# Both halves of a chunk's diagonal products in a row, cumulative sums in column halves, and a new order of steps

## The chip, the cores and the metric

The kernel runs on one core of one Trainium2 chip. The metric is the device time of one execution, in microseconds (us). The program is one launch; the weights are laid out beforehand with their contracted dimension first.

## What is computed

One block of a network on an input of 2 batches x 2048 tokens x 512 features, all in float32. A small product of a condition with `wmod` gives shifts, scales and gates for each batch. Then come a mixer and a feed-forward, each on a normalized and modulated input and added back through a gate:

```python
h = layernorm(x) * (1 + ca) + sa
x = x + ga * mixer(h)
h = layernorm(x) * (1 + cb) + sb
x = x + gb * (silu(h @ Wg) * (h @ Wu)) @ Wd     # integer weights, widened and scaled

# mixer: zxbcdt = h @ W_in.T; x, B, C through a causal convolution of 4 taps and silu
Y_diag = einsum('bcln,bcsn,bhcls,bcshp->bclhp', C, B, L, X)    # L = exp of differences of cumsum(dt*A)
Y_off  = einsum('bcln,bchpn,bhcl->bclhp', C, states, exp(A_cumsum))
y = (Y_diag + Y_off + Dp * X) * silu(z);  y = rmsnorm(y) * norm_w;  out = y @ W_out.T
```

The mixer has 16 heads of 64 features, a state of 128 per head, and an inner width of 1024. The kernel works in chunks of 128 tokens.

## The kernel before

**Stages.** `mixer_stage` handles 4096 tokens in 16 tiles of 256 tokens (two chunks of 128), the two batches taking turns. The first step (`first`) runs the setup and the projections of tile 0. Then come 15 turns, `turn(n, b)` for n = 1 to 15; each projects tile n (calls guarded by `own`), finishes tile u = n - 1 (guarded by `bef`) and prepares the input of tile n + 1 (guarded by `nxt`). The last tile is finished in `drain`, mixed with the first products of the feed-forward, and the feed-forward follows (`FeedForward`).

**Order.** Each engine has its own list of steps, written out by hand in `first`, `turn` and `drain` of its block, and runs it strictly in that order. Between engines there are semaphores; each step waits for counts (`wait(eng, sem, n, per, c)` waits for n * per + c).

**TensorE's list in a turn.** `scores_G` (the B, C products of both chunks, one bank `small`), `project_zdt` (2), `project_tile` (10; 12 float32r products of 256 columns each), `project_z` (4), and for the chunks c = 0, 1 of tile u: `transpose_x`, `transpose_B`, two `y_off` (a half f of 8 heads each, bank `yoff`), two `y_diag` (bank `ydiag`), two `states` (bank `state`), `transpose_g`, `project_out`. `cumulate` multiplies dt*A with a triangle and with ones for the cumulative sums. A full-precision float32 product is issued as two MATMUL instructions.

**y_diag** already works in column halves: each head's 128 output rows are computed as two products of 64 rows, at the tile positions (0, 0) and (0, 64), 32 instructions for a half of 8 heads. Both halves go to the bank `ydiag`, so the second half waits until VectorE has read the first (`read_ydiag`, L1124 to L1128). In the old list `project_tile` 0 and 1 stand between the halves of chunk 0; `cumulate`, `project_tile` 8, `project_out`, `project_tile` 9 and `y_off(1, 1)` between those of chunk 1. `y_diag(0, 0)` and both last `y_diag` of the chunks stand behind or before steps of full width.

**VectorE's list in a turn.** `mask_G`, four `scores` (decay times masked B, C products, 128x1024), four `read_yoff`, `decay_S`, `read_ydiag` and `read_state`, two `decay_X`, two `gate`, 30 `conv` (three taps of ten tiles), 17 small steps of `softplus` that end in `dtA`, `sums` (reads `cumulate`'s result), `stats`, `norm`, `split_h`, `low_g`, and four `diff` (8 operations each on the broadcast sums). `states(c, 1)` on TensorE waits for `read_state(c, 0)`; `cumulate` waits for `dtA`; `project_zdt(n + 1, c)` waits for `split_h`.

**ScalarE** evacuates banks (`evac_tile`, `evac_x`, `evac_g`, `silu_z`, `scale_out`) and computes silu and exp. **GpSimd** multiplies X with D and adds the residual. **SyncE's queue** stores the sums to memory and broadcasts them back over the partitions, 1 MB for each chunk (L548); the broadcast of chunk 1 stands behind the store of x1 of chunk 0 and the load of the next residual rows, which follows `project_out(0)`.

## Time and profile before

| | |
|---|---|
| median of 3 runs | 1459.25 us (1459.07 to 1463.02) |
| the profiled execution | 1463.41 us, of which the span is 1461.7 us |
| TensorE busy | 1430.2 us |
| VectorE busy | 1116.2 us |
| ScalarE busy | 637.5 us |
| mean granted TensorE clock | 0.996 |
| first step and setup | 0 to 74.54 us of the span |
| the 15 turns | 74.54 to 927.21 us |
| drain and feed-forward | 927.21 to 1461.7 us |

Busy time is the union of an engine's instructions. Matmul ends are modelled, and matmuls overlap, so the time of a block of them is best read from the start of its first to the start of the next block's first. In lines of the timeline, equal neighbours are merged (x12), and a bracket gives the engine's idle time before them and who ended it. A turn here goes from one `scores_G` (L1481) to the next.

### The profile page before, as it was taken

To read this page: it belongs to the slowest core of one execution; us is meant where nothing else is said; L and a number is where in the kernel's file an instruction comes from. 1 tells how busy PE (TensorE), PEld (TensorE's weight loads), DVE (VectorE), ACT (ScalarE), POOL (GpSimd) and SP (SyncE) were. 2 spreads that over 40 slices of the span, in tenths; PEclk is the share of its full clock that TensorE was granted. 3 is DMA by queue.
4 is the path that set the end of the run, shared out by engine and by line. 5 is a ranking of instruction groups with operands and counts; after the bars stand their busy time and mean duration, and the time that the engine had idled before them with its cause. 6 is when DMAs were issued, how large, how long until landed. Compare 5 with 4: busy or idle time off the path is not lost.

```text
span 1461.7 us, 25392 instructions
## 1 busy us (share of the span) xinstructions
PE 1430.2 (98%) x9369; PEld 1146.0 (78%) x9369; DVE 1116.2 (76%) x2521; ACT 637.5 (44%) x1300; POOL 298.7 (20%) x335
## 2 busy tenths in 40 slices
PE   7999999999999999999999999999999999999998
PEld 3677787787887887877777778779888888888887
DVE  4799998998998999999998999857536455364632
ACT  4565565575575565564655654422212011120210
POOL 1012223213212312322322132121110211101101
PEclk9999999999999999999999999999999999999999
DMA  9413213212222222132132132702210202112010
GB/s 320 151 37 131 88 45 123 87 52 96 94 88 95 68 100 95 41 135 100 39 131 81 51 116 70 292 15 80 73 59 28 87 14 73 39 49 87 8 51 30
DMA packets 56409, 124.99 MB, mean 86 GB/s; under 512 B 6438, under 2 KB 10066, under 8 KB 52188
## 3 DMA queue, kind: packets, MB, share of 16 engines
q1 hardware_dynamic: 55744, 123.27, 24.1%
q8 instruction: 77, 1.26, 0.4%
q14 instruction: 48, 0.39, 0.1%
q10 hardware_dynamic: 540, 0.07, 0.0%
HBM read 97.62 MB, written 25.69 MB: 84 GB/s over the span
## 4 chain that ended last, share of the span: by engine, by line
PE 70%; DVE 19%; issue 7%; POOL 1%; DMA 1%; ACT 1%; DVEq 0%; POOLq 0%; SPq 0%
PE bank L2032 18%; PE bank L1443 17%; PE bank L2062 9%; PE bank L1594 7%; PE bank L1592 6%; DVE xBC L987 5%; PE bank L1532 3%; DVE decay L1079 2%; PE bank L1557 2%; DVE state L1121 2%; PE bank L325 2%; DVE y L1134 1%; DVE X_D L1127 1%; PE bank L1544 1%; DVE X L1097 1%
## 5 line engine op out<-in xcount | busy, mean ns | idle before, releaser
L1867 ACT ACTIVATE silu_gate<-bank,params 128x512 f32<-128x512 f32 (+1 forms) x99 | 63.5, 642 | 366.0 <-PE bank L2032 343.8
L987 DVE SCALAR_TENSOR_TENSOR xBC<-conv_in,wconv,xBC 128x256 f32<-128x256 f32 x480 | 211.9, 474 | 3.3 <-ACT xBC L697 0.4
L1939 DVE SCALAR_TENSOR_TENSOR hidden<-bank,params,silu_gate 128x512 f32<-128x512 f32 (+1 forms) x99 | 68.3, 690 | 125.6 <-PE bank L2032 124.4
L2062 PE MATMUL bank<-W_down,hidden_high 128*128 128x512 f32 x374 | 139.1, 390 | 0.0
L606 POOL TENSOR_TENSOR X_D<-X,Drow 128x1024 f32<-128x1024 f32 x32 | 62.7, 1961 | 352.9 <-ACT X_D L781 315.5
L2032 PE MATMUL bank<-ff_h_high,W_gate 128*128 128x512 f32 (+1 forms) x352 | 132.3, 380 | 0.0
L2032 PE MATMUL bank<-ff_h_high,W_up 128*128 128x512 f32 (+1 forms) x352 | 131.1, 376 | 0.3 <-DVE hidden L1939 0.3
L2032 PE MATMUL bank<-ff_h_low,W_gate 128*128 128x512 f32 (+1 forms) x352 | 131.0, 376 | 0.0
L2032 PE MATMUL bank<-ff_h_low,W_up 128*128 128x512 f32 (+1 forms) x352 | 131.0, 376 | 0.0
L2062 PE MATMUL bank<-W_down,hidden_low 128*128 128x512 f32 x330 | 128.5, 389 | 0.0
L1443 PE MATMUL bank<-h_high,W_in_high 128*128 128x256 f32 x640 | 124.7, 317 | 0.1
L1594 PE MATMUL bank<-W_out,gT 128*128 128x512 f32 x256 | 115.0, 592 | 0.0
L1062 DVE TENSOR_SCALAR decay<-decay,sums 128x128 f32<-128x128 f32 x512 | 106.5, 283 | 0.0
L1443 PEld LDWEIGHTS bank<-h_high,W_in_high 128*128 128x128 f32 x640 | 89.0, 190 | 21.5 <-issue 18.5
L1859 POOL TENSOR_TENSOR ff_x_resid<-ff_branch,ff_x_resid 128x512 f32<-128x512 f32 x32 | 41.3, 1291 | 298.2 <-DVE ff_branch L1970 292.8
L1443 PE MATMUL bank<-h_high,W_in_low 128*128 128x256 f32 x640 | 101.5, 280 | 0.0
L1443 PE MATMUL bank<-h_low,W_in_high 128*128 128x256 f32 x640 | 101.4, 280 | 0.0
L696 ACT ACTIVATE conv_in<-bank 128x256 f32<-128x256 f32 x160 | 61.0, 381 | 88.2 <-PE bank L1443 88.2
L1970 DVE TENSOR_TENSOR ff_branch<-bank,gate_row 128x512 f32<-128x512 f32 x32 | 22.1, 690 | 100.7 <-PE bank L2062 100.7
L1544 PEld LDWEIGHTS bank<-X,decay 128*64 128x64 f32 x2048 | 65.0, 138 | 38.2 <-issue 27.7
L1079 DVE TENSOR_TENSOR decay<-decay,G_masked 128x1024 f32<-128x1024 f32 x64 | 91.9, 1436 | 0.9 <-ACT decay L770 0.4
L697 ACT ACTIVATE xBC<-bank,params,wconv 128x256 f32<-128x256 f32 x160 | 90.2, 564 | 0.0
(196 smaller groups left out, 3276.0 us busy)
## 6 DMA issues: line engine op xcount, KB each, us to landing
decay<-sums_scratch SPq DMA_DIRECT2D x32, 1024.0 KB, 5.2
wq_rows<-wqT SPq DMA_DIRECT2D x33, 256.0 KB, 4.8
widened_scratch<-wq_rows SPq DMA_DIRECT2D x33, 256.0 KB, 3.4
x_tile<-x SPq DMA_DIRECT2D x32, 256.0 KB, 3.1
x_resid<-x SPq DMA_DIRECT2D x32, 256.0 KB, 2.9
x_scratch<-x_resid SPq DMA_DIRECT2D x32, 256.0 KB, 3.0
ff_x_resid<-x_scratch SPq DMA_DIRECT2D x32, 256.0 KB, 4.5
out<-ff_x_resid SPq DMA_DIRECT2D x32, 256.0 KB, 2.0
```

Of the source, the lines that this page charges most:

```text
L697: nc.scalar.activation(A.xc[b][:, m, :], ps[:, 0:SC], ACT.Identity, bias=A.bconv[:, m:m + 1], scale=A.wconv[:, m, 3:4]).then_inc(a_emptied, 1)
L987: nc.vector.scalar_tensor_tensor(A.xc[b][:, m, :], A.raw[:, m, j:j + SC], A.wconv[:, m, j:j + 1], A.xc[b][:, m, :], ALU.mult, ALU.add).the ...
L1062: last = nc.vector.tensor_scalar(A.L[c][:, h, :], A.L[c][:, h, :], A.s3[:, c * H + h:c * H + h + 1], 0.0, ALU.subtract, ALU.min)
L1079: nc.vector.tensor_tensor(x, x, A.Gm[:, c, :].unsqueeze(1).broadcast_to([P, HH, P]), ALU.mult) \
L1443: mm = nc.tensor.matmul(out, lhs(wp, ap), rhs(wp, ap), start=(i == 0), stop=(i == last))
L1544: mm = nc.tensor.matmul(ydiag[s, h * HD:(h + 1) * HD], A.L[c][:, g, s], A.X[:, g * HD:(g + 1) * HD], start=True, stop=True, tile_position= ...
L1592: nc.tensor.matmul(ps[:], gT[gp][:, k, :], Wo[wp][:, k, :], start=(k == 0 and i == 0), stop=False)
L1594: mm = nc.tensor.matmul(ps[:], A.gT[:, k, :], A.Wo[:, k, :], start=False, stop=(k == KI - KH - 1))
L1867: self.nc.scalar.activation(B.sg[m % 2][:, 0:size], self.gates[m % 2][:, 0:size], ACT.Silu, scale=self.T.sgate[:, m:m + 1]).then_inc(self. ...
L1939: nc.vector.scalar_tensor_tensor(hid, self.ups[m % 2][:, 0:size], self.T.sup[:, m:m + 1], B.sg[m % 2][:, 0:size], ALU.mult, ALU.mult).then ...
L2032: mm = nc.tensor.matmul(ps[:, 0:self.TURNS[t][2]], W[:, k, m * P:(m + 1) * P].bitcast(dt), self.h(t, a, k).bitcast(dt), start=(k == 0 and ...
L2062: mm = nc.tensor.matmul(self.downs[c % 2][:], self.hidden_tile(t, a, m)[:, s].bitcast(dt), B.Wd[:, m, :].bitcast(dt), start=(m == 0 and a ...
```

## The change

Three things are done at once.

1. `column_halves` is a helper that issues a product as two of 64 output rows. `y_diag` uses it as before; `cumulate` now uses it for its first two products too, so these have 8 MATMUL instructions of 64 rows in place of 4 of 128 rows. The third product of `cumulate` stays as it was.
2. The second half of `y_diag` writes to the bank `state` instead of `ydiag`, except in `drain`. It waits for the state's reads instead of for `read_ydiag` of the first half, and `states(c, 0)` waits until that bank has been read. Both halves of a chunk now follow each other directly; behind those of chunk 0 stands `transpose_B`, behind those of chunk 1 stands `cumulate`.
3. The lists of steps of TensorE, VectorE and ScalarE have a new order, in `first` and in `turn`. In the turn, `states(1, 1)` on TensorE moves behind `project_out(1)`. On VectorE, `scores(0, 1)` and `scores(1, 0)` move forward, `read_yoff(0, 1)` moves behind `read_ydiag(0, 0)`, `decay_S(0, 1)` behind `gate(0)`, most of the softplus steps stand without other work between them, `sums` moves forward, `norm(0)` and `norm(1)` stand together behind `gate(1)`, `conv` 9's first two taps move among the `diff`, `decay_S(1, 1)` moves just before `read_state(1, 0)`, and `read_state(1, 1)` to the end. On ScalarE, `evac_zdt(0)` comes before `evac_x(0)`, `exp_dt` behind `evac_tile` 2, `evac_x(1)` behind `evac_tile` 5, `measure(0)` behind `silu_z(1)`, and `exp_sums` just before the last `exp_decay`. In `first`, ScalarE scales the rest of W_out (`wout_scale`) before `silu_z(0)` instead of behind `silu_z(1)`, `silu_q` comes earlier and `widen_second` behind the last silu; TensorE's `gate_rows` come before `project_z(0)`, and its second `section` directly behind the first. The queues of SyncE and GpSimd keep their lists.

```diff
+
+
+def column_halves(nc, out, lhsT, rhs):
+
+    for i in (0, P // 2):
+        s = slice(i, i + P // 2)
+        mm = nc.tensor.matmul(out[s, :], lhsT[:, s], rhs, start=True, stop=True, tile_position=(0, i))
+    return mm
...
+        self.section(pe, 1)
         pe.wait_ge(self.const_step, 6)
         self.turn_cols(pe, 0)
-        self.section(pe, 1)
         transpose_ln()
         self.turn_cols(pe, 1)
         pe.wait_ge(self.win_low, 1)
...
+    def ydiag_bank(n, f):
+
+        return state if f and n != N else ydiag
+
...
                 wait(dve, yoff_done, u, 2 * NC, 2 * c + f + 1)
+                wait(dve, e3_done, u, 1, 1)
                 nc.vector.tensor_tensor(heads(A.S[1 - b], f), heads(A.S[1 - b], f), e3(1, c, f),
...
-        def read_ydiag(u, c, f):
+        def read_ydiag(n, u, c, f):
             wait(dve, ydiag_done, u, 2 * NC, 2 * c + f + 1)
             wait(dve, XD_done, u, NC, c + 1)
-            nc.vector.tensor_tensor(A.XD[:, f * W:(f + 1) * W], ydiag[:, 0:W], A.XD[:, f * W:(f + 1) * W],
+            nc.vector.tensor_tensor(A.XD[:, f * W:(f + 1) * W], ydiag_bank(n, f)[:, 0:W], A.XD[:, f * W:(f + 1) * W],
                                     ALU.add).then_inc(ydiag_read, 1)
 
...
@@ -1252,123 +1260,133 @@
             if bef:
                 mask_G(u)
                 scores(u, 0, 0)
+                scores(u, 0, 1)
                 read_yoff(n, u, b, 0, 0)
-                scores(u, 0, 1)
+                decay_S(u, b, 0, 0)
+                scores(u, 1, 0)
+            if own:
+                conv(n, b, 0, 0)
+            if bef:
+                read_ydiag(n, u, 0, 0)
                 read_yoff(n, u, b, 0, 1)
-                decay_S(u, b, 0, 0)
+                decay_X(n, u, 0)
+            if own:
+                dt_first(n, b)
+            if bef:
+                read_ydiag(n, u, 0, 1)
+            if own:
+                conv(n, b, 1, 0)
+            if bef:
+                gate(n, u, b, 0)
+            if own:
+                conv(n, b, 0, 1)
+                conv(n, b, 1, 1)
+            if bef:
                 decay_S(u, b, 0, 1)
-                read_ydiag(u, 0, 0)
...
-            nc.tensor.matmul(small[:, 0:NC * H], A.triu[:], a, start=True, stop=True)
-            nc.tensor.matmul(small[:, NC * H:2 * NC * H], A.ones[:], a, start=True, stop=True)
+            column_halves(nc, small[:, 0:NC * H], A.triu[:], a)
+            column_halves(nc, small[:, NC * H:2 * NC * H], A.ones[:], a)
             mm = nc.tensor.matmul(small[0:NC * H, 2 * P:3 * P], a, A.triu[:], start=True, stop=True)
             mm.then_inc(cs_done, 1)
...
@@ -1536,14 +1554,16 @@
             wait(pe, M_done, u, 2 * NC, 2 * c + f + 1)
             t_wait(pe, t_emptied, n, ("x", c, f), 1)
 
-            wait(pe, ydiag_read, u, 2 * NC, 2 * c + f)
+            ps = ydiag_bank(n, f)
+            if ps is state:
+
+                wait(pe, S_step, u, 4 * NC, 4 * c)
+            else:
+                wait(pe, ydiag_read, u, 2 * NC, 2 * c + f)
             for h in range(HH):
                 g = f * HH + h
-                for i in (0, P // 2):
-                    s = slice(i, i + P // 2)
-                    mm = nc.tensor.matmul(ydiag[s, h * HD:(h + 1) * HD], A.L[c][:, g, s],
-                                          A.X[:, g * HD:(g + 1) * HD], start=True, stop=True,
-                                          tile_position=(0, i))
+                mm = column_halves(nc, ps[:, h * HD:(h + 1) * HD], A.L[c][:, g, :],
+                                   A.X[:, g * HD:(g + 1) * HD])
             mm.then_inc(ydiag_done, 1)
 
         def states(n, u, c, f):
@@ -1553,6 +1573,7 @@
             if f:
                 wait(pe, S_step, u, 4 * NC, 4 * c + 3)
             else:
+                wait(pe, ydiag_read, u, 2 * NC, 2 * c + 2)
                 wait(pe, S_step, u, 4 * NC, 4 * c)
             nc.tensor.matmul(state[:, 0:W], A.Btok[:], A.X[:, f * W:(f + 1) * W],
                              start=True, stop=True).then_inc(state_done, 1)
...
             u = before(n)
@@ -1636,56 +1657,52 @@
                 scores_G(n, u, b)
             if own:
                 project_zdt(n, 0)
+                project_zdt(n, 1)
             if bef:
                 y_off(u, b, 0, 0)
                 transpose_x(n, u, b, 0)
             if own:
-                project_zdt(n, 1)
+                project_tile(n, 0)
             if bef:
                 y_off(u, b, 0, 1)
                 y_diag(n, u, 0, 0)
-            if own:
-                project_tile(n, 0)
+                y_diag(n, u, 0, 1)
+                transpose_B(n, u, b, 0)
+            if own:
                 project_tile(n, 1)
             if bef:
-                y_diag(n, u, 0, 1)
+                transpose_x(n, u, b, 1)
             if own:
                 project_tile(n, 2)
-            if bef:
-                transpose_B(n, u, b, 0)
-            if own:
                 project_tile(n, 3)
             if bef:
                 states(n, u, 0, 0)
-                transpose_x(n, u, b, 1)
             if own:
                 project_tile(n, 4)
+                project_tile(n, 5)
             if bef:
                 states(n, u, 0, 1)
             if own:
-                project_tile(n, 5)
+                project_tile(n, 6)
             if bef:
                 transpose_B(n, u, b, 1)
             if own:
-                project_tile(n, 6)
+                project_tile(n, 7)
             if bef:
                 transpose_g(n, u, 0)
             if own:
-                project_tile(n, 7)
+                project_tile(n, 8)
             if bef:
                 y_off(u, b, 1, 0)
                 y_diag(n, u, 1, 0)
+                y_diag(n, u, 1, 1)
             if own:
                 cumulate(n)
-                project_tile(n, 8)
             if bef:
                 project_out(n, u, 0)
+                y_off(u, b, 1, 1)
             if own:
                 project_tile(n, 9)
-            if bef:
-                y_off(u, b, 1, 1)
-                y_diag(n, u, 1, 1)
-            if own:
                 project_z(n, 0)
                 project_z(n, 1)
             if bef:
@@ -1699,8 +1716,8 @@
             if own:
                 project_z(n, 3)
             if bef:
+                project_out(n, u, 1)
                 states(n, u, 1, 1)
-                project_out(n, u, 1)
 
         def drain(project):
 
```

## Rows read from the trace of the kernel before

**Rows 1.** The page's busy time of each engine, share of the span and instructions.

```profile
PE 1430.2 (98%) x9369; PEld 1146.0 (78%) x9369; DVE 1116.2 (76%) x2521; ACT 637.5 (44%) x1300; POOL 298.7 (20%) x335
```

**Rows 2.** Stretches: busy time and instructions of each engine, granted clock (PEclk), DMA share and rate.

```profile
0.00:74.54 74.54, 60.73 (x308) 38.22 (x308) 46.98 (x128) 41.13 (x76) 6.58 (x23) 0.95 0.66 232
74.54:133.09 58.55, 57.89 (x428) 46.21 (x429) 53.30 (x127) 35.44 (x75) 10.56 (x12) 0.97 0.24 80
...
528.14:584.36 56.22, 56.06 (x429) 44.57 (x428) 52.22 (x126) 32.98 (x71) 13.97 (x14) 1.00 0.25 86
```

**Rows 3.** Waits of TensorE: total us, times, longest.

```profile
PE bank L1481 <- ACT xBC L704: 4.0, 1, 4.0
...
PE bank L1491 <- DVE dtA L1038: 2.6, 15, 0.2
PE bank L1557 <- DVE state L1147: 2.4, 6, 0.5
```

**Rows 4.** TensorE's timeline in one turn, around the y_diag of chunk 0.

```profile
533.32 1.02 PE L1532 MATMUL bank<-state,xBC 128*128 128x512 f32 x2
534.27 1.15 PE L1544 MATMUL bank<-X,decay 128*64 128x64 f32 x32
535.35 0.74 PE L1443 MATMUL bank<-h_high,W_in_high 128*128 128x256 f32 x4
535.94 0.64 PE L1443 MATMUL bank<-h_low,W_in_high 128*128 128x256 f32 x4
536.41 0.64 PE L1443 MATMUL bank<-h_high,W_in_low 128*128 128x256 f32 x4
...
537.83 0.63 PE L1443 MATMUL bank<-h_high,W_in_low 128*128 128x256 f32 x4
538.39 1.15 PE L1544 MATMUL bank<-X,decay 128*64 128x64 f32 x32
```

**Rows 5.** TensorE's timeline in that turn, around cumulate.

```profile
552.79 1.15 PE L1544 MATMUL bank<-X,decay 128*64 128x64 f32 x32
554.10 0.41 PE L1491 MATMUL bank<-dtA,triu 128*128 128x32 f32 x2 [0.16 <-DVE dtA L1038]
554.35 0.39 PE L1492 MATMUL bank<-dtA,ones 128*128 128x32 f32 x2
554.66 0.41 PE L1493 MATMUL bank<-triu,dtA 128*32 128x128 f32 x2
555.00 0.74 PE L1443 MATMUL bank<-h_high,W_in_high 128*128 128x256 f32 x4
555.58 0.64 PE L1443 MATMUL bank<-h_low,W_in_high 128*128 128x256 f32 x4
```

**Rows 6.** VectorE's timeline in the same turn.

```profile
534.38 0.69 DVE L1114 TENSOR_TENSOR y<-bank,exp_sums 128x512 f32<-128x512 f32 x1 [0.66 <-PE bank L1532]
534.99 1.64 DVE L1121 TENSOR_TENSOR state<-state,exp_sums 128x512 f32<-128x512 f32 x2
...
537.47 1.22 DVE L1079 TENSOR_TENSOR decay<-decay,G_masked 128x1024 f32<-128x1024 f32 x1
538.61 1.92 DVE L987 SCALAR_TENSOR_TENSOR xBC<-conv_in,wconv,xBC 128x256 f32<-128x256 f32 x4
...
553.86 0.19 DVE L1038 TENSOR_TENSOR dtA<-softplus,negA 128x32 f32<-128x32 f32 x1
...
572.83 0.68 DVE L1153 TENSOR_TENSOR gT_low<-bank,gT_high 128x512 fp32r<-128x512 f32 x1
...
578.75 1.65 DVE L1062 TENSOR_SCALAR decay<-decay,sums 128x128 f32<-128x128 f32 x8
...
582.66 0.69 DVE L977 TENSOR_TENSOR h_low<-X_D,h_high 128x512 fp32r<-128x512 f32 x1
```

**Rows 7.** The queue of SyncE in that turn: the broadcast of chunk 1.

```profile
571.57 0.44 SPq L548 DMA_DIRECT2D decay<-sums_scratch  x1
```

**Rows 8.** ScalarE's timeline in the first step, before project_z(0)'s evacuation.

```profile
61.78 0.60 ACT L712 ACTIVATE silu_z<-bank 128x512 f32<-128x512 f32 x1 [1.95 <-PE bank L1443]
```

More of the change, by code:

```diff
@@ L1263, in turn @@
             if bef:
-                scores(u, 1, 0)
+                read_ydiag(n, u, 0, 1)
             if own:
-                conv(n, b, 0, 0)
-                conv(n, b, 0, 1)
-                conv(n, b, 0, 2)
                 conv(n, b, 1, 0)
             if bef:
-                decay_X(n, u, 0)
-                read_ydiag(u, 0, 1)
+                gate(n, u, b, 0)
[3 more added lines that the diff above has]
+            if bef:
+                decay_S(u, b, 0, 1)
             if own:
@@ L1300, in turn @@
             if own:
+                softplus(n, 2)
+                conv(n, b, 2, 0)
+                conv(n, b, 3, 1)
+                softplus(n, 3)
+            conv(n, b, 3, 2)
+            if own:
+                softplus(n, 4)
+            softplus(n, 5)
+            softplus(n, 6)
+            softplus(n, 7)
+            if own:
+                softplus(n, 8)
                 softplus(n, 9)
@@ L1304, in turn @@
             if bef:
-                low_g(n, u, 0)
+                read_state(u, b, 0, 1)
             if own:
                 softplus(n, 12)
+                conv(n, b, 2, 1)
             if bef:
@@ L1311, in turn @@
                 softplus(n, 13)
+            if bef:
+                low_g(n, u, 0)
+            if own:
+                conv(n, b, 2, 2)
                 softplus(n, 14)
+                conv(n, b, 5, 0)
                 conv(n, b, 4, 0)
[L1314 removed]
+            if bef:
+                decay_S(u, b, 1, 0)
+                read_yoff(n, u, b, 1, 0)
             if nxt:
                 stats(after(n), 1)
+            if own:
+                conv(n, b, 4, 1)
             if bef:
[L1318 to L1319 removed]
+                read_ydiag(n, u, 1, 0)
             if own:
[L1321 removed]
                 conv(n, b, 4, 2)
+                conv(n, b, 6, 0)
+                sums(n)
                 conv(n, b, 5, 1)
[L1324 removed]
                 conv(n, b, 5, 2)
+                conv(n, b, 7, 0)
                 conv(n, b, 6, 1)
[L1327 removed]
             if bef:
[L1329 removed]
+                decay_X(n, u, 1)
             conv(n, b, 7, 1)
+            if bef:
+                read_yoff(n, u, b, 1, 1)
             if own:
                 conv(n, b, 6, 2)
[L1333 removed]
                 conv(n, b, 7, 2)
             if bef:
[L1336 to L1339 removed]
+                read_ydiag(n, u, 1, 1)
                 gate(n, u, b, 1)
+            if own:
+                conv(n, b, 8, 0)
             if nxt:
                 norm(after(n), n, 0)
[L1343 to L1346 removed]
                 norm(after(n), n, 1)
@@ L1349, in turn @@
                 top_square(n)
+                conv(n, b, 9, 0)
+                conv(n, b, 8, 1)
             if bef:
@@ L1352, in turn @@
             if own:
-                conv(n, b, 9, 0)
+                diff(n, 0, 0)
                 conv(n, b, 8, 2)
+                diff(n, 0, 1)
+                conv(n, b, 9, 1)
             if bef:
+                decay_S(u, b, 1, 1)
                 read_state(u, b, 1, 0)
             if own:
-                conv(n, b, 9, 1)
-                diff(n, 0, 0)
-                diff(n, 0, 1)
+                diff(n, 1, 0)
                 conv(n, b, 9, 2)
-                diff(n, 1, 0)
+            if nxt:
+                split_h(after(n), n, 0)
+            if own:
+                tails(n, b)
+            if nxt:
+                split_h(after(n), n, 1)
+            if own:
+                exact_flag(n)
+                diff(n, 1, 1)
             if bef:
                 read_state(u, b, 1, 1)
-            if nxt:
-                split_h(after(n), n, 0)
-                split_h(after(n), n, 1)
-            if own:
-                tails(n, b)
-                exact_flag(n)
-                diff(n, 1, 1)
         def drain():
```

214 lines of the change are left out of this document (87 added, 127 removed).

## Prediction

> **What bounds the kernel now.** I read the page's totals first. TensorE is busy for 1430.2 of 1461.7 us, VectorE for 1116.2 [rows 1]. Matmul ends are modelled, so 98% does not say that TensorE could not be faster; it says that there are few holes, and that what counts is how far apart the starts are. Next came the stretches [rows 2]: the change touches the first step (74.54 us) and 15 turns of some 56.2 us; drain and feed-forward keep their order. In an undisturbed turn (528.14 to 584.36) TensorE is busy for 56.06 of 56.22 us and VectorE for 52.22, so a second engine is close behind. Then the waits of TensorE [rows 3]: only three concern us. `scores_G` of the first turn waits 4.0 us for the last silu, `cumulate` waits in all 15 turns for `dtA` (2.6 us in all), and `states(0, 1)` in six turns for `read_state(0, 0)` (2.4 us). The wait at `cumulate` is small but telling: in that part of the turn VectorE sets the pace and has no slack. Last I read the turn's timeline start by start [rows 4, 5], since a price of changing from one form of product to another shows only there.
>
> **Merging the halves of y_diag.** One half takes 1.08 us from its first start to the next block's (534.27 to 535.35), 34 ns for each of 32 instructions [rows 4]. The tile behind it needs 0.59 us for its first four products where its next four need 0.47: leaving column halves costs 0.12. The group of four that ends at 538.39 took 0.56 for 0.47: entering costs 0.09. A turn now enters four times and leaves four times (one leaving falls into `cumulate`). Afterwards it enters twice and leaves twice (towards `transpose_B`, and inside `cumulate`). Without the one inside `cumulate`, that is 4 x 0.09 + 3 x 0.12 = 0.72 before and 2 x 0.09 + 0.12 = 0.30 after: 0.42 saved in a turn. Leaving towards a float32 transpose is not in the trace; I price it like leaving towards a tile, and its bounds are 0 and the 0.23 seen between y_diag and `cumulate` (554.10 less 553.87) [rows 5]. The other bank costs nothing between the halves by my count; the bound above is one more entry, 0.09 each, or 0.18. So 0.13 to 0.54, and I take 0.42.
>
> **The sums in column halves.** From the end of y_diag's own 1.08 us (553.87) to the next tile's start (555.00) `cumulate` takes 1.13, and the tile behind it starts 0.11 slower (0.58 for 0.47): 1.24 [rows 5]. Of this 0.16 is the wait for `dtA`. Afterwards: eight instructions in the form that the array is already in, at y_diag's 34 ns, 0.27; leaving, 0.12; the third product 0.34 as now (554.66 to 555.00); the slower start behind it 0.11. That is 0.84, saving 0.40. The nearest row for a column half is y_diag's, same weights of 128x64 and 64 moving columns instead of 32. From the other side, if each of the eight kept the 0.12 that one of the present four takes (554.10 to 554.35 for two), they would need 1.0 and the whole 1.55: 0.31 lost. A gain beyond 0.40 is excluded because no column-half instruction in the trace starts sooner than 34 ns after the last.
>
> The Trainium skill ("TensorEngine Tiling (Array Packing)", Instruction Overhead) speaks against this edit: about 60 cycles for each matmul however few columns move, and no tiling of what is already small. At 2.4 GHz that estimate is 25 ns each, so doubling four instructions would add 0.10 us to a turn instead of saving. The trace has 34 ns for a half and 122 for a full one, which leaves room for both; by the page the sum below would be 0.50 x 15 = 7.5 us smaller. No row of before has a half with 32 moving columns.
>
> Both parts are on TensorE's own path, so they count 15 times if nothing else stops it: (0.42 + 0.40) x 15 = 12.3 us.
>
> **Whether VectorE lets it.** TensorE's turn would be about 55.4 us, VectorE's work stays at 52.2. So totals fit, and the places where one waits for the other decide.
>
> *dtA to cumulate.* Before: VectorE goes from `read_yoff(0, 1)` at 534.38 to the end of `dtA` at 554.05 without a hole, 19.67 us [rows 6], and TensorE from `y_off(0, 1)` at 533.32 to 554.10, 20.8 [rows 4, 5]. After, the anchor is y_diag(0, 0). Behind its read VectorE has the same list without one `decay_S` (0.8), `scores(1, 0)` (1.14) and one `conv` (0.4), which now stand earlier: 17.3. Softplus steps 4 to 11 now have nothing between them and each waits for the last; I add an estimated 0.4. With y_diag's 1.08 and 0.2 for the semaphore (`y_off`'s result at 533.32 + 0.86 was read at 534.38) `dtA` is there after 19.0. TensorE from y_diag(0, 0) to `cumulate`: the 20.8 less `y_off` (0.95), plus a fourth y_diag (1.08), less switches and wait (0.4): 20.5. Slack 1.5 us where it was below zero; the 0.16 is gone, as counted. *states(0, 1)*: TensorE's list has two tiles between `states(0, 0)` and `states(0, 1)` instead of `transpose_x` and one tile, 0.6 us more, and `read_state(0, 0)` is not later. The six waits, at most 0.5 each, go: 2.4 us. *y_off(1, 1) to transpose_g(1)*: `decay_S`, `decay_X` and the sums have been moved out of VectorE's piece, so about 1.5 us of slack come in.
>
> *The tail.* Behind `low_g(1)` VectorE needed from 572.83 to 583.35 for `split_h` [rows 6], 10.5 us; the new list there has `decay_S(1, 1)` more, a `conv` and a `read_state` less, about the same. TensorE has the same steps as before between `transpose_g(1)` and the next turn, two of them swapped. So the spare time stays what it was: from 583.35 to the `project_zdt` behind the turn's start at 584.36 [rows 2], at least 1.0 and with `scores_G` some 1.4 us. `read_state(1, 1)` at the very end is asked for by nobody before the next second half of y_diag, 8 us later.
>
> **The first step.** `scores_G` waits 4.0 us for a silu. Before, ScalarE idles 1.95 us for `project_z(0)` [rows 8] and is then busy to the end; now `wout_scale` fills that hole and `silu_q` and `widen` leave the piece. I take 2.0 of the 4.0; bounds 0 and 4.0. The first turn takes 58.55 us against 56.22, at a granted clock of 0.97 [rows 2], behind that hole; if the hole became short enough, up to 1.6 more could return. I take 0.
>
> **Sum.** 12.3 + 2.4 + 2.0 = 16.7 us. Against its own execution 1463.4 becomes 1446.7; that execution stood 4.2 above the median, so against the median 1459.25 the time is 1442.6.
>
> **Rivals.** *The halves save nothing* (each instruction as dear as now): 0.31 lost instead of 0.40 gained, 10.7 us less: gain 6.0, 1453.2. For it: no row has the form. Against: y_diag's. Chance 0.12.
>
> *VectorE takes the pace.* It is busy 52.2 of what would be 55.4, and its places of waiting for TensorE (0.66 before `read_yoff(0, 1)` [rows 6]) show that lists meet. If each turn stays at 56.2 because waits of 0.8 appear, only 2.4 + 2.0 remain: 1454.9. Against: the slacks above. Chance 0.16.
>
> *Slower: the second broadcast.* SyncE's queue issues it at 571.57 [rows 7], 43.4 us into the turn, behind store and load that follow `project_out(0)`; that product now ends about 1.3 us later in the turn, behind one more y_diag. VectorE needs its data for `diff(1, 0)` at 578.75 [rows 6], 7.2 us after issue, and the new list asks about 50 us into the turn, 5.3 after issue. If it lands more than 1.4 us late the split is late and TensorE waits at `project_zdt`. It decides when the wait passes 1.1 us a turn, so from 2.5 us late on; at 4 us late it costs 2.6 x 15 = 39 against 16.7: 1481. Against: `sums` stand 3 us earlier, so the first broadcast is out of the way. Chance 0.04.
>
> *Nothing moves much*, gains eaten by small stalls that I can't place: within 4 us of before. Chance 0.06.
>
> **How the numbers follow.** My forecast has 0.62. 0.3% is 4.4 us, about what a measurement of this kernel tells from no change. Forecast and first rival are faster; the second stands just at the bound and gives 0.08 to faster, 0.06 to the same and 0.02 to slower; the last gives 0.03 to the same, 0.01 to faster, 0.02 to slower. Faster 0.83, same 0.09, slower 0.08. The range: below, the whole 4.0 of the first wait, the 1.6 of the clock and other small stalls, 23 us of gain: 1436; above, the first rival: 1453.
>
> **What would show it.** y_diag should appear as one block of 64 instructions in 2.16 us; the tile behind `transpose_B` without the 0.12; `cumulate`'s eight instructions within 0.3 us and no wait for `dtA`; no wait of L1557's group for `read_state`; turns of 55.2 to 55.6 us; `scores_G` of the first turn waiting about 2 us. I am wrong if turns stay at 56.2, if a new row for `split_h`, `diff` or an evacuation stands among TensorE's waits, or if the eight instructions take over 0.5 us.

## The result, and the profile after

The changed kernel takes 1434.4 us (median of 4 runs, 1434.02 to 1434.95), the kernel before 1460.69 in 4 runs beside it (1459.07 to 1463.02): a ratio of 0.9817, with an interval of 0.9802 to 0.9833. The direction is as predicted. The size is not: 1442.6 was forecast, with 1436 as the lower end.

The page's busy time, share and instructions (before: [rows 1]):

```profile
PE 1408.6 (98%) x9433; PEld 1133.9 (79%) x9433; DVE 1141.1 (80%) x2521; ACT 642.7 (45%) x1300; POOL 284.4 (20%) x335
```

The stretches, in the order first step, first turn, an undisturbed turn (before: [rows 2]):

```profile
0.00:69.83 69.83, 59.67 (x312) 37.07 (x312) 44.12 (x127) 40.45 (x76) 6.80 (x23) 0.98 0.69 246
69.83:126.85 57.02, 55.46 (x433) 44.10 (x434) 53.71 (x127) 36.22 (x75) 10.64 (x12) 1.00 0.24 84
566.29:621.13 54.84, 54.84 (x433) 43.95 (x432) 53.89 (x126) 33.32 (x72) 13.26 (x14) 1.00 0.25 88
```

The span went from 1461.7 to 1432.9 us, 28.8 less. The medians differ by 26.3, since before's profiled execution, 1463.4, stands 2.7 above the median of its four runs. From these stretches and the starts of `scores_G` the 28.8 divide into:

| stretch | before | after | difference |
|---|---|---|---|
| first step | 74.54 | 69.83 | -4.7 |
| 15 turns, 15 times an undisturbed one | 843.5 | 822.6 | -20.9 |
| what single turns take above that | 9.2 | 5.0 | -4.2 |
| drain and feed-forward | 534.5 | 535.5 | +1.0 |

An undisturbed turn is 1.39 us shorter, where 0.82 was predicted. Busy TensorE time, a sum of modelled ends, fell from 56.06 to 54.84 in it and fills it. VectorE, which should have stayed at 52.2, shows 53.89.

The waits of TensorE after (total, times, longest), those that stand highest behind the wait of 5.4 for the first weights. They are to be held against [rows 3]:

```profile
PE bank L1593 <- DVE gT_low L1161: 3.0, 2, 1.6
PE bank L1461 <- DVE h_low L984: 2.4, 2, 1.3
PE bank L1499 <- ACT xBC L716: 1.8, 1, 1.8
```

Nothing in this list occurs once a turn. The 15 waits of `cumulate` for `dtA` and the six of `states(0, 1)` for `read_state` are gone; `scores_G` (now L1499) waits 1.8 us, not 4.0.

TensorE's timeline around the two halves of chunk 0 (before: [rows 4]):

```profile
572.91 1.02 PE L1550 MATMUL bank<-state,xBC 128*128 128x512 f32 x2
573.87 2.08 PE L56 MATMUL bank<-X,decay 128*64 128x64 f32 x64
575.88 0.33 PE L1534 MATMUL bank<-ident,xBC 128*128 128x128 f32 x1
575.97 0.71 PE L1461 MATMUL bank<-h_high,W_in_high 128*128 128x256 f32 x4
576.52 0.63 PE L1461 MATMUL bank<-h_low,W_in_high 128*128 128x256 f32 x4
```

64 instructions take 2.01 us from the first start to the next block's, where before two halves took 1.08 each, with 34 ns an instruction. Split at the 33rd instruction, the first half takes 0.98 us and the second 1.03.

The same around `cumulate` (before: [rows 5]):

```profile
590.92 1.02 PE L1550 MATMUL bank<-state,xBC 128*128 128x512 f32 x2
591.88 2.09 PE L56 MATMUL bank<-X,decay 128*64 128x64 f32 x64
593.79 0.26 PE L56 MATMUL bank<-dtA,triu 128*64 128x32 f32 x4
593.88 0.29 PE L56 MATMUL bank<-dtA,ones 128*64 128x32 f32 x4
594.10 0.41 PE L1511 MATMUL bank<-triu,dtA 128*32 128x128 f32 x2
594.43 0.50 PE L1613 MATMUL bank<-W_out_high,gT_high 128*128 128x512 f32 x1
```

The first four column halves take 0.09 us to the next start, some 22 ns each; all eight take 0.31 with the leaving in it, where four of full width took 0.56. The 64 of y_diag, with column halves behind them as well, need only 1.91: 0.98 for the first half and 0.93 for the second. So 0.93, 29 ns an instruction, is y_diag's own time for a half that has column halves on both sides. A full-width block in front adds 0.05 to it, one behind adds 0.10.

VectorE and GpSimd, three lines of one and one of the other (before: [rows 6]):

```profile
572.71 2.92 DVE L1086 TENSOR_TENSOR decay<-decay,G_masked 128x1024 f32<-128x1024 f32 x1
...
592.80 0.18 DVE L1045 TENSOR_TENSOR dtA<-softplus,negA 128x32 f32<-128x32 f32 x1
...
607.58 0.42 DVE L1148 TENSOR_TENSOR y<-y,z_dt 128x256 f32<-128x256 f32 x1
```

```profile
572.42 2.13 POOL L618 TENSOR_TENSOR X_D<-X,Drow 128x1024 f32<-128x1024 f32 x1 [3.06 <-ACT X L748]
```

`dtA` ends at 592.98 and `cumulate` starts at 593.79: 0.8 us of slack. `gate(1)` ends at 608.0 and `transpose_g(1)` starts at 608.09: 0.1. And `scores(1, 0)` takes 2.92 us where the same operation takes 1.22 [rows 6], beside GpSimd's product of X and D, which started 0.3 us before it.

### The profile page after: what moved, and what is told of

Its sections match the earlier page's. It is cut to its first block, busy times and chain, and to the rows that moved or that the text cites. A ratio compares the mean times of both kernels' runs of the same rounds, so it can differ in the third digit from the quotient of the medians.

```text
span 1432.9 us, 25628 instructions
## 1 busy us (share of the span) xinstructions
PE 1408.6 (98%) x9433; PEld 1133.9 (79%) x9433; DVE 1141.1 (80%) x2521; ACT 642.7 (45%) x1300; POOL 284.4 (20%) x335
## 4 chain that ended last, share of the span: by engine, by line
PE 87%; issue 5%; DVE 3%; ACT 2%; POOL 1%; DMA 1%; POOLq 0%; SPq 0%; DVEq 0%; ACTq 0%
PE bank L1461 26%; PE bank L2049 18%; PE bank L2079 9%; PE bank L1615 7%; PE bank L1613 6%; PE bank L56 5%; PE bank L1550 4%; PE bank L1578 3%; PE bank L1527 2%; PE bank L1593 2%; PE bank L333 2%; PE bank L1451 1%; PE bank L2030 1%; DVE decay L1069 1%; DVE xBC L994 1%
## 5 line engine op out<-in xcount | busy, mean ns | idle before, releaser
L994 DVE SCALAR_TENSOR_TENSOR xBC<-conv_in,wconv,xBC 128x256 f32<-128x256 f32 x480 | 240.6, 526 | 5.2 <-ACT xBC L709 4.4
L1069 DVE TENSOR_SCALAR decay<-decay,sums 128x128 f32<-128x128 f32 x512 | 124.5, 316 | 0.0
L1086 DVE TENSOR_TENSOR decay<-decay,G_masked 128x1024 f32<-128x1024 f32 x64 | 99.8, 1578 | 0.6
L1615 PEld LDWEIGHTS bank<-W_out,gT 128*128 128x128 f32 x256 | 48.4, 189 | 48.8 <-issue 46.0
```

The costliest lines, as they stand in the source:

```text
L994: nc.vector.scalar_tensor_tensor(A.xc[b][:, m, :], A.raw[:, m, j:j + SC], A.wconv[:, m, j:j + 1], A.xc[b][:, m, :], ALU.mult, ALU.add).the ...
L1069: last = nc.vector.tensor_scalar(A.L[c][:, h, :], A.L[c][:, h, :], A.s3[:, c * H + h:c * H + h + 1], 0.0, ALU.subtract, ALU.min)
L1086: nc.vector.tensor_tensor(x, x, A.Gm[:, c, :].unsqueeze(1).broadcast_to([P, HH, P]), ALU.mult) \
L1615: mm = nc.tensor.matmul(ps[:], A.gT[:, k, :], A.Wo[:, k, :], start=False, stop=(k == KI - KH - 1))
```

## The experiments

Each was timed beside the kernel before (1460.8 to 1461.3 us there), and its ratio is to that. "After" is the changed kernel, 1434.4. A turn is an undisturbed one: 56.23 before, 54.84 after.

### e1_full_sums: the sums back at full width

```diff
@@ cumulate, in after
-            column_halves(nc, small[:, 0:NC * H], A.triu[:], a)
-            column_halves(nc, small[:, NC * H:2 * NC * H], A.ones[:], a)
+            nc.tensor.matmul(small[:, 0:NC * H], A.triu[:], a, start=True, stop=True)
+            nc.tensor.matmul(small[:, NC * H:2 * NC * H], A.ones[:], a, start=True, stop=True)
```

> The changed kernel with the sums in full width again; the rest as changed. Theory A (the blocks of TensorE alone explain the 1.39 us that a turn lost): y_diag and sums behind it took 1.326 + 0.244 + 0.317 + 0.336 + 0.112 = 2.34 us before, less the 0.16 wait 2.18, and take 1.69 now, so each turn grows by 0.48, to 55.3, and the kernel by 7.3 us to about 1441.7. Theory B (my recorded prices hold, and the rest came from hidden pacing by VectorE that the new lists removed): 0.24 a turn without the wait, 3.6 us, about 1438.

1439.65 us, ratio 0.9862 (0.9845 to 0.9878), turns of 55.19, 0.35 longer: between the two theories (0.48 and 0.24). TensorE's timeline around `cumulate`:

```profile
593.81 2.09 PE L56 MATMUL bank<-X,decay 128*64 128x64 f32 x64
595.83 0.41 PE L1509 MATMUL bank<-dtA,triu 128*128 128x32 f32 x2
596.07 0.39 PE L1510 MATMUL bank<-dtA,ones 128*128 128x32 f32 x2
596.39 0.41 PE L1511 MATMUL bank<-triu,dtA 128*32 128x128 f32 x2
```

The halves are worth 0.35 us a turn: the products take 0.56 against 0.31, and y_diag's 64 take 2.02 against 1.91 because full width follows them. This run also shows what the wait for `dtA` cost. From y_diag to `cumulate`, here without a wait, the last half takes 1.03 us, as it does ahead of a transpose. In before `y_diag(1, 0)` takes 1.31 to `cumulate` (552.79 to 554.10) and 1.08 wherever it doesn't wait, so the wait delayed TensorE by 0.23, or 0.24 in the median of the undisturbed turns. The 0.16 in the bracket of [rows 5] is only the idle time behind a modelled end. So of the turn's 1.39 us 0.35 belong to the halves, 0.24 to the wait for `dtA`, and 0.80 to the merging. Counted block by block, the merging shows 0.41 around chunk 0's y_diag and 0.35 around chunk 1's; the last 0.04 are spread over the turn.

### e10_apart_first_chunk: one tile back between the halves of chunk 0

```diff
@@ TensorE's turn, in after
                 y_diag(n, u, 0, 0)
+            if own:
+                project_tile(n, 1)
+            if bef:
                 y_diag(n, u, 0, 1)
                 transpose_B(n, u, b, 0)
             if own:
-                project_tile(n, 1)
+                project_tile(n, 2)
             if bef:
                 transpose_x(n, u, b, 1)
             if own:
-                project_tile(n, 2)
                 project_tile(n, 3)
```

> The changed kernel with project_tile(1) between the two halves of y_diag of chunk 0 and tile 2 behind transpose_B; chunk 1, banks and the other lists as changed, and no step nearer to a wait of VectorE or to an evacuation than 0.5 us. It is the price of one more stay in column halves alone. Theory A: 0.10 in y_diag's last part, 0.12 behind it, 0.09 ahead: 0.31 a turn, turns of 55.15, 4.7 us slower than the changed kernel, about 1439. Theory B (my recorded prices): 0.21 a turn, 3.2 us, about 1437.6.

1444.79 us, 0.9888 (0.9871 to 0.9904), turns of 55.51: 0.67 longer, more than either expectation. TensorE's timeline:

```profile
579.67 1.15 PE L56 MATMUL bank<-X,decay 128*64 128x64 f32 x32
580.75 0.74 PE L1461 MATMUL bank<-h_high,W_in_high 128*128 128x256 f32 x4
581.32 0.63 PE L1461 MATMUL bank<-h_low,W_in_high 128*128 128x256 f32 x4
581.79 0.63 PE L1461 MATMUL bank<-h_high,W_in_low 128*128 128x256 f32 x4
582.35 1.15 PE L56 MATMUL bank<-X,decay 128*64 128x64 f32 x32
583.43 0.33 PE L1534 MATMUL bank<-ident,xBC 128*128 128x128 f32 x1
```

Both halves are back at 1.08. The tile between them takes 1.60, where a tile behind a tile takes 1.42 in after: leaving 0.10 (0.57 for 0.47) and entering 0.09 (0.56 for 0.47). With what y_diag's two halves gain (0.10 and 0.05) that is 0.34 for one more stay in column halves, with small differences in the blocks behind it 0.35. Another 0.27 us stand at `states(0, 1)` and the tiles around it, which take 3.94 from start to start and 3.67 in after. The list of waits shows nothing there, since it counts a wait from the modelled end of what stood before, but the starts do, here VectorE's `read_state(0, 0)` and TensorE's `states(0, 1)`:

```profile
590.23 0.69 DVE L1155 TENSOR_TENSOR state<-bank,state 128x512 f32<-128x512 f32 x1
```

```profile
591.07 1.10 PE L1578 MATMUL bank<-X,B_rows 128*128 128x512 f32 x2
```

`states(0, 1)` starts 0.15 us after `read_state(0, 0)` ends in every turn (590.92 and 591.07 here), the same distance as in those turns of before that list this wait; in after it is mostly 0.50. `transpose_B(1)` starts 0.14 to 0.15 after ScalarE's first `evac_x(1)` in every turn; in after it is mostly 0.30. A constant distance means that the hand-over sets the start. The last 0.05 of the turn's 0.67 are in `transpose_B(1)` itself and in `transpose_g(1)`, which starts 0.06 after `gate(1)` ends. So moving one tile forward used up the room at two places, one of VectorE's and one of ScalarE's, where the expectation had counted on 0.5 us.

### e4_apart_new_lists and e8_lists_alone: both pairs apart

e4 puts tile 1 between the halves of chunk 0 and tile 8 between those of chunk 1; e8 is e4 with e1's edit as well.

```diff
@@ TensorE's turn, in after
                 y_diag(n, u, 0, 0)
+            if own:
+                project_tile(n, 1)
+            if bef:
                 y_diag(n, u, 0, 1)
...
-            if own:
-                project_tile(n, 8)
             if bef:
                 y_off(u, b, 1, 0)
                 y_diag(n, u, 1, 0)
+            if own:
+                project_tile(n, 8)
+            if bef:
                 y_diag(n, u, 1, 1)
```

> The changed kernel with one project_tile between the two halves of y_diag in each chunk (tile 1 and tile 8, moved by one place); banks, waits and the other engines' lists as changed. Theory A: each stay in column halves costs 0.12 behind it, 0.09 ahead of it, and 0.10 that is hidden in the last part of y_diag's own 1.08; two more stays a turn cost 0.62 us, 9.3 in all: turns of 55.45, about 1443.7. Theory B: 0.21 for each, 0.42 a turn, 6.3 in all: about 1440.7. y_diag followed by a tile should read 1.08 again, followed by itself 0.98.

> Both of the above: halves apart and sums in full width, so that of the change the new lists of steps (and the bank) are left. Theory A: the turns go back to 54.84 + 0.48 + 0.62 = 55.9 to 56.2 us, without the extra stalls of single turns, and the first step keeps its gain: about 1451, 9 to 10 us under the kernel before. Theory B: the lists carry about half of the gain in the turns: about 1445.

1465.09 (1.003, 1.0018 to 1.0043) and 1470.52 (1.0068, 1.0051 to 1.0085): both far above every expectation, with turns of 56.85 and 57.19. The waits of e4:

```profile
PE bank L1550 <- DVE state L1155: 11.9, 15, 0.8
```

Tile 8 had covered VectorE's `read_state(0, 1)`. With it moved behind, `y_off(1, 0)` is asked for 1.4 us earlier and waits 0.79 us in each turn. So these two don't price the merging. Around the halves e4's blocks show 0.34 for each of the two further stays (a tile between the halves takes 1.60 and 1.61, and a tile behind a tile 1.42), in line with e10; and e8 is 0.34 a turn longer than e4, which repeats e1's 0.35 in another surrounding. What the miss does show is that two tiles moved by one place in the new list lose 30.7 us, more than all that the change gains. Tile 8 has most of it: e4 takes 20.3 us more than e10, which moves tile 1 alone, and one stay is 5 of them.

### e3_merge_old_lists, e9_merge_and_halves_old_lists, e2_half_sums_old_lists: the parts without the new order

```diff
@@ e3, in before
+    def ydiag_bank(n, f):
+
+        return state if f and n != N else ydiag
...
                 y_diag(n, u, 0, 0)
+                y_diag(n, u, 0, 1)
             if own:
                 project_tile(n, 0)
                 project_tile(n, 1)
-            if bef:
-                y_diag(n, u, 0, 1)
-            if own:
                 project_tile(n, 2)
...
                 y_diag(n, u, 1, 0)
+                y_diag(n, u, 1, 1)
             if own:
                 cumulate(n)
...
                 y_off(u, b, 1, 1)
-                y_diag(n, u, 1, 1)
@@ e2, in before; e9 is e3 with this
-            nc.tensor.matmul(small[:, 0:NC * H], A.triu[:], a, start=True, stop=True)
-            nc.tensor.matmul(small[:, NC * H:2 * NC * H], A.ones[:], a, start=True, stop=True)
+            column_halves(nc, small[:, 0:NC * H], A.triu[:], a)
+            column_halves(nc, small[:, NC * H:2 * NC * H], A.ones[:], a)
```

> The kernel before with the halves of y_diag of each chunk in a row (second half in the state's bank) and nothing else: sums in full width, VectorE's and ScalarE's lists and first as before. Theory A (VectorE set the pace between y_off(0, 1) and the sums): the 0.31 saved in chunk 0 turns into a longer wait for dtA, but y_diag(1, 1) fills that wait and leaves the later part of the turn: 0.8 us a turn less, 55.4, and with some of the single stalls left about 1449. Theory B (prices of 0.21): 0.42 a turn, about 1454. If VectorE's old list paces the whole turn: no gain, 1460.

> As the last one, with the first two products of the sums in column halves too. If TensorE is the bound there, another 0.35 a turn (what the full width cost in the changed kernel), 5.2 us less: about 1443 to 1444; the distance of that to the changed kernel, some 9 us, is what the new lists are worth: 4.7 in the first step and the single stalls of turns. If VectorE's old list sets the pace, the halves give nothing here and the lists carry more.

> The kernel before with only the first two products of the sums in column halves. They wait for dtA in all turns there, so the leaving price and the wait stay where they are; only the two products themselves shrink, 0.244 + 0.317 to 0.307, and y_diag's last 0.10 goes into the wait: 0.25 to 0.35 a turn if the shorter piece reaches the end of the turn, 3.8 to 5.2 us, about 1456. If VectorE's list paces the whole turn in the kernel before: nothing, 1460.

e3: 1472.19 us, 1.0074 (1.0058 to 1.0091), turns of 57.15. e9: 1468.07, 1.0046 (1.0029 to 1.0063), turns of 56.81. e2: 1459.78, 0.9993 (0.9983 to 1.0004). All missed what was expected; e2's 1460 was named there for a VectorE that paces the whole turn, but e2's undisturbed turn did get shorter. The waits of e3:

```profile
PE bank L1581 <- DVE y L1144: 13.9, 15, 0.9
PE bank L1566 <- DVE X_D L1131: 7.2, 15, 0.7
```

The merging saves on TensorE there as well (halves of 0.98 and 1.03 in chunk 0), and no wait for `dtA` is listed, but TensorE now asks sooner for what VectorE's old list does late: `transpose_g(1)` waits 0.93 us a turn for `gate(1)`, and `states(0, 0)` 0.48 for the read of the second half, which now stands in its bank. So the merging alone makes the kernel slower, and so does the merging with the halves. In e2 the sums' two products take 0.36 us in place of 0.56 and the undisturbed turn loses those 0.20, while the wait for `dtA` stays (2.7 us, 15 times) and some turns show single stalls (57.03 to 59.01); no difference is left.

### e5_old_first: the first step in its old order

```diff
@@ ScalarE's first, in after (the other lists of setup and first likewise)
-                evac_tile(n, b, 2)
...
+                evac_tile(n, b, 2)
...
-            setup.wout_scale(act)
...
+            setup.wout_scale(act)
@@ TensorE's setup
-        self.section(pe, 1)
         pe.wait_ge(self.const_step, 6)
         self.turn_cols(pe, 0)
+        self.section(pe, 1)
```

> The changed kernel with setup and first step in the old order; turns as changed. If the first step's own 4.7 us (74.54 to 69.83 until the first scores_G) come from its order: scores_G again near 74.3 with a wait of about 4 us for the last silu, and 4 to 6 us slower than the changed kernel, about 1439 to 1440, since the first turn runs at a lower clock again. If ScalarE's list in the turns had a part in it, less.

1436.16 us, 0.9834 (0.9817 to 0.985), turns of 54.84: 1.8 us above after, where 4 to 6 were expected. `scores_G` waits 4.0 us again and comes at 73.06, 3.2 later than in after; drain and feed-forward are 1.0 shorter (534.5). The two intervals overlap, so the 1.8 are not clear of noise. The rest of the gain is the turns'. Against e9, which has all but the new lists of the turns and of the first step, it is 32 us less: that is what the new order of the turns is worth once the halves are merged.

### e11_vector_plus_one and e12_vector_plus_two: more work on VectorE

```diff
@@ VectorE's turn, in after, behind softplus(n, 13) and ahead of dtA; once in e11, twice in e12
+                    nc.vector.bn_stats(A.pad[:], A.Wo[:, 0, :]).then_inc(pad_done, 1)
```

> The changed kernel with two more bn_stats of 128x512 on VectorE in each turn before dtA, 1.4 us, whose result nobody reads. VectorE is busy for 53.6 to 53.9 of a turn's 54.84 us without a hole. If it sets the pace of the turns now, each grows by 1.4, 21 us: 1455. If TensorE does, only what goes beyond the 0.8 us between the end of dtA and the start of the sums is lost, 0.6 a turn, 9 us: 1443; less if single operations that now wait beside GpSimd's shrink in turn.

> The changed kernel with one more bn_stats (0.72 us) on VectorE in each turn before dtA. Two of them cost 1.2 us a turn: 0.5 at the sums and 0.5 at transpose_g(1), which waits for gate(1). If VectorE has next to no room before gate(1): about 0.5 a turn, 7 to 8 us, 1442. If there is 0.7 of room: nothing.

e12: 1452.16 us, 0.9937 (0.9921 to 0.9954), turns 1.21 longer for 1.44 us of work. e11: 1442.38, 0.9876 (0.9859 to 0.9892), turns 0.62 longer for 0.72. The waits of e12:

```profile
PE bank L1599 <- DVE y L1149: 5.7, 15, 0.7
...
PE bank L56 <- DVE dtA L1046: 5.3, 14, 0.8
```

In e11 only the first of the two is there (3.8 us, 14 times). So 0.1 us of VectorE's work is free in a turn, the slack read at `gate(1)`; whatever goes beyond it is paid almost in full. e12 came nearer to the theory that VectorE paces (1455) than to that of 0.8 us of slack (1443), which looked at `dtA` alone.

### e13_short_gpsimd and e14_short_gpsimd_vector_plus_two: less of GpSimd

e13 leaves out all but the first 64 columns of GpSimd's product of X and D, of its product with the gate and of its residual sum, so only its time means something. e14 adds e12's two operations to e13.

```diff
@@ GpSimd, in after
-            nc.gpsimd.tensor_tensor(A.XD[:].rearrange("p (h d) -> p h d", h=H),
+            nc.gpsimd.tensor_tensor(A.XD[:, 0:64].rearrange("p (h d) -> p h d", h=1),
...
-            nc.gpsimd.tensor_tensor(A.ob[:], A.ob[:], T.gate_row[1 - b][:], ALU.mult).then_inc(out_step, 1)
+            nc.gpsimd.tensor_tensor(A.ob[:, 0:64], A.ob[:, 0:64], T.gate_row[1 - b][:, 0:64], ALU.mult).then_inc(out_step, 1)
```

> The changed kernel with GpSimd's large operations (X times D, gate, residual) on 64 columns instead of 1024 and 512, the rest of these products left out. In each turn single operations of VectorE that start beside them last 1.0 to 1.7 us longer (scores(1, 0) 2.9 instead of 1.2, a conv 1.5 instead of 0.5, a diff 1.4 instead of 0.3). If the two engines hold each other up, these fall back to 1.2, 0.5 and 0.3. Since TensorE sets the pace of the turns: within 0.1 us a turn of 54.84, 1433 to 1434.5. If VectorE did: up to 3.5 us a turn less, far under 1420.

> The last one with the 1.4 us more on VectorE before dtA. If the operations beside GpSimd eat VectorE's room, the room is back: turns near 54.9, 1434 to 1436, where the load alone costs 1452. If the room was missing for another reason, as slow as with the load alone.

e13: 1431.55 us, 0.98 (0.9784 to 0.9817), turns of 54.82. e14: 1433.42, 0.9811 (0.9795 to 0.9828), turns of 54.93, with no wait for `dtA` or `gate(1)` in the list. The turns are as expected; the times are 1.5 and 0.6 us under the expected ranges; a shorter drain and feed-forward, 534.3 and 534.2 us against 535.5, is part of that. An undisturbed turn of e13, then VectorE's `scores(1, 0)`:

```profile
564.92:619.74 54.82, 54.82 (x433) 44.03 (x432) 49.87 (x126) 33.50 (x73) 5.99 (x14) 1.00 0.25 88
```

```profile
570.66 1.22 DVE L1086 TENSOR_TENSOR decay<-decay,G_masked 128x1024 f32<-128x1024 f32 x1
```

VectorE's list is the same and its busy time fell from 53.89 to 49.87; `scores(1, 0)` is back at 1.22. So 4.0 us of VectorE's time in a turn were operations lengthened beside GpSimd's. That the turn is 54.82 all the same shows that TensorE sets the pace, and that e12's 1.21 us shrink to 0.11 shows where VectorE's room had gone.

## Why the prediction was right in direction and wrong in size

**What bounds the kernel: right.** TensorE's starts set the turn. With 4.0 us of VectorE's busy time gone (e13) the turn is still 54.82 us.

**Merging the halves: the step that failed.** Predicted 0.42 a turn, measured 0.80 (before less e1 is 1.04, and 0.24 of that is the wait). Over 15 turns the missing 0.38 is 5.7 us, the largest part of what the forecast was too high by (8.2). The step that failed is the price of a stay in column halves, 0.21 us: 0.09 for entering and 0.12 for leaving. Both of these terms held. What was left out is in the prediction's own first sentence on this part: it took 1.08 us, 34 ns for each of 32 instructions, as y_diag's own time. That time is 0.93, and the other 0.15 belong to the stay. The trace of before shows it when its block of 32 is cut open by narrow windows (first two and next eight; last eight, last two and the tile behind them):

```profile
534.27 0.28 PE L1544 MATMUL bank<-X,decay 128*64 128x64 f32 x2
534.38 0.40 PE L1544 MATMUL bank<-X,decay 128*64 128x64 f32 x8
...
535.02 0.40 PE L1544 MATMUL bank<-X,decay 128*64 128x64 f32 x8
535.20 0.23 PE L1544 MATMUL bank<-X,decay 128*64 128x64 f32 x2
535.35 0.39 PE L1443 MATMUL bank<-h_high,W_in_high 128*128 128x256 f32 x1
```

Six instructions inside take 0.18 us (535.02 to 535.20), 0.06 for two. The first two take 0.11 and the last two 0.15: 0.05 and, within the rounding, 0.10 more. So a stay costs 0.35 us (0.09 + 0.05 + 0.10, and 0.11 behind it, read as 0.12 in [rows 4]), and e10 and e4 measure 0.34 for one more. In chunk 0 one of two stays is gone (0.35), and the other now ends towards a transpose, which costs 0.05 behind y_diag instead of 0.11: 0.41 together. In chunk 1 one stay is gone, 0.35. The transpose was priced like a tile, at 0.12, within stated bounds of 0 to 0.23; the upper bound of the whole, 0.54, was too low because the hidden 0.15 was no part of it. The same mean of 34 ns was used to exclude a larger gain at the sums, and there too it was a mean over a block with both its edges, not the distance inside.

The Trainium skill ("TensorEngine Tiling (Array Packing)", Key Properties) says that a change of the tiling mode drains TensorE. The 0.35 us for a stay agree with it; it gives no duration.

**The other bank: right.** It costs nothing between the halves: the first half takes 0.98 with the other bank behind it, and the 0.05 above 0.93 stand at its start.

**The sums in column halves: right in kind, too small.** Predicted 0.40 with 0.16 of the wait in it; measured 0.35 (e1) and 0.24 for the wait, 0.59. The prediction took the wait as the bracket gives it, and the 0.23 from the end of y_diag's 1.08 to `cumulate` as a bound for leaving; e1 shows that all of that 0.23 was the wait. The eight instructions were put at 0.27 and 0.12 for leaving, and take 0.31 with the leaving in it. The first rival, that a half is as dear as a whole, is out: the first four take some 22 ns each, and with the full products the kernel takes 5 us more. By the Trainium skill's rule ("TensorEngine Tiling (Array Packing)", Instruction Overhead) the doubling would have cost 0.10 us a turn. The 22 ns are close to the 25 that it gives for an instruction, but the full-width ones that they replace take 122 to 160, taken in pairs. Its advice against taking a tiling factor from a small dimension is not tested here: what is halved is the 128 output rows, and the small dimension is the 32 moving columns.

**Whether VectorE lets it: right in the outcome, wrong in its reckoning.** No wait took the place of those removed. But slacks of 1.5 us at `dtA` and 1.5 at `transpose_g(1)` were predicted, and 0.8 and 0.1 are there. A shorter TensorE turn takes some: the turn shrank by 0.57 more than reckoned. VectorE's work, counted as constant at 52.2, became 53.9: three operations in a turn run over 1 us long, each beside a large GpSimd operation: `scores(1, 0)` with 2.92 for 1.22, a `conv` with 1.51 for 0.48 and a `diff` with 1.42 for 0.28. That is 3.9 us. Two more `conv` take 0.70 and 0.87, and e13, where GpSimd's operations are short but still there, gives 4.0 back in all. The rival in which VectorE takes the pace had a chance of 0.16 and did not come, but only 0.1 us kept it off. In before's timeline the same thing could be read from its first two `scores`, 2.25 and 1.71 us for 1.22, each begun during one of GpSimd's two operations on the residual; the prediction took such times as they were:

```profile
529.24 2.25 DVE L1079 TENSOR_TENSOR decay<-decay,G_masked 128x1024 f32<-128x1024 f32 x1
...
532.01 1.71 DVE L1079 TENSOR_TENSOR decay<-decay,G_masked 128x1024 f32<-128x1024 f32 x1
```

```profile
529.10 1.30 POOL L623 TENSOR_TENSOR branch<-branch,gate_row 128x512 f32<-128x512 f32 x1 [7.36 <-ACT branch L788]
530.48 2.15 POOL L626 TENSOR_TENSOR x_resid<-branch,x_resid 128x512 f32<-128x512 f32 x1
```

**states(0, 1): right.** The wait is gone (2.4 us). Single stalls fell by 4.2 us; the other 1.8 are turns longer for reasons that the profile doesn't name and that vary from kernel to kernel (e13 has all turns but the first and the last at 54.82).

**The first step: half right.** The wait went from 4.0 to 1.8 us, 2.2 for 2.0 predicted. The stretch is 4.7 shorter. Another 1.1 is a shorter wait for `h_low` (3.5 to 2.4); the first step of e2, e3 and e9, which is before's, took 73.4 to 73.8 us rather than 74.54, so up to 1.1 is this execution's. The first turn now runs at a granted clock of 1.00, where it had 0.97, but what it takes above an undisturbed turn went only from 2.3 to 2.2 us: the 1.6 that the prediction held out did not come, and its choice of 0 was right. Drain and feed-forward gave 1.0 back, which had not been foreseen. It stands at one place, early in the drain:

```profile
PE bank L2019 <- issue: 0.7, 1, 0.7
```

After, e1, e4, e8 and e10 have this wait and 535.5 to 535.7 us there; before, e3, e5, e9 and e11 to e14 don't have it and take 534.2 to 534.6, with the same lists in the drain; e2, without it, takes 535.2. What TensorE waits for there the profile doesn't name, and why only some kernels have it stays open.

**The slower rival: out.** No wait of `diff` for a broadcast shows in the turn: VectorE's timeline has no hole in 54.84 us but short gaps between its operations.

**In sum:** 12.3 + 2.4 + 2.0 = 16.7 was predicted; the profiled executions show 20.9 + 4.2 + 4.7 - 1.0 = 28.8. Of the 12.1 more, 8.6 come from the turns (5.7 of the merging, 2.9 of the sums and the wait before them), 2.7 from the first step, 1.8 from single stalls, and the drain took 1.0. The prediction took 4.2 off for its profiled execution, where four runs put it at 2.7 above the median.

**What it passed over:** it priced the new order by the waits that it removes, 2.4 us. e3 and e9 show another side: with the old lists the merged halves make new waits, listed with 1.4 us a turn, and the kernel is slower than before. The new order is what makes the gain possible.

## What to carry to other kernels

A block's time from its first start to the next block's holds part of the cost of entering and leaving its form. Read the pace of its instructions inside the block, with windows that cut it open, and count what the first and last ones take beyond that as the price of the form. A listed wait counts from a modelled end, so a start may be late by more than the list says, or be late without being listed; hold starts against the end of what they wait for. When the leading engine gets shorter, read the slack of the second engine at every hand-over and let its operations that overlap the third engine's be as long as they can become: totals of 52 in 55 us hid a slack of 0.1. A saving on the leading engine counts only when the lists of the others are early enough; try the part alone in the old lists before praising it.

## What the runs showed of the hardware

- One stay in column halves between products of full width costs TensorE 0.35 us: 0.09 in front, 0.05 at its first instructions, 0.10 at its last and 0.11 behind. Towards a float32 transpose the leaving is 0.15 (0.10 and 0.05) instead of 0.21. One more stay measured 0.34 in e10 and e4.
- Inside such a block a product of 64 output rows starts every 29 ns on average with 64 moving columns (0.93 us for 32), and every 22 ns with 32 (0.09 us for four).
- When TensorE waits for VectorE's read of the bank `state`, it starts 0.15 us after that read ends (before and e10).
- VectorE's `scores`, with two operands in SBUF, waits for the whole of a GpSimd operation that started before it. `scores(1, 0)` started at 572.71 and GpSimd's product ran until 574.55: 1.84 us of waiting and 1.22 of work would be 3.06, and 2.92 are there. The Trainium skill ("SBUF — State Buffer", "SBUF: two separate sides") calls the pair of ports that the two engines share an exclusive lock, held for the whole instruction by whoever starts first; the trace agrees within 0.14 us.
